# The last two passes of a graph network: selecting by products against turning rows and scanning

## The reference

```python
def _gcn_layer(x, W, b, src, dst, norm, n_nodes):
    xt = x @ W
    msg = xt[src] * norm[:, None]
    agg = jax.ops.segment_sum(msg, dst, num_segments=n_nodes)
    return jax.nn.relu(agg + b)
norm = edge_weight * jax.lax.rsqrt(deg_out[src] * deg_in[dst] + EPS)
h6 = _gcn_layer(h5_all, W6, b6, src, dst, norm, N_NODES)
h7 = _gcn_layer(h6, W7, b7, src, dst, norm, N_NODES)
out = h7 @ Wp + bp
```

## Time and profile before

| | us |
|---|---|
| median of 3 runs | 5989.73 |
| profiled execution, span from the first to the last instruction | 5993.1 |
| fifth pass, POOL's first gather to the start of the last pass | 412.1 |
| last pass, to the end | 588.7 |
| PE busy over the span | 4608.6 (77%) |
| DVE busy | 4603.5 (77%) |
| POOL busy | 3500.3 (58%) |
| ACT busy | 2965.7 (49%) |

### The profile page before, as it was taken

The page is one execution under the profiler, slowest core; times in us unless marked ns, Lnnn a source line. Parts: engine busy times, 40 slices in busy tenths (PEclk is TensorE's granted clock), DMA queues, the critical chain, the costliest instruction groups (busy, mean ns, idle before and its releaser), DMA issues. The chain is left out here.

```text
span 5993.1 us, 77451 instructions
## 1 busy us (share of the span) xinstructions
PE 4608.6 (77%) x21160; PEld 3351.9 (56%) x21160; DVE 4603.5 (77%) x13478; ACT 2965.7 (49%) x7524; POOL 3500.3 (58%) x3009
## 2 busy tenths in 40 slices
PE   3888888888884888865777778888857674887887
PEld 3666666666663666643565545555534443665555
DVE  5888888888886888847999647777768887985554
ACT  2777777777772444432444435555545552331111
POOL 3555445454524767728888278777725433546777
PEclk9999999999996999987888889999978887998998
DMA  3666666667663444425777535555536774554444
GB/s 119 239 242 247 237 243 241 244 242 244 240 236 128 125 123 129 128 71 174 256 243 250 200 110 155 147 151 155 154 103 217 249 241 151 169 159 132 140 156 130
DMA packets 651621, 1096.83 MB, mean 183 GB/s; under 512 B 88390, under 2 KB 471814, under 8 KB 651069
## 3 DMA queue, kind: packets, MB, share of 16 engines
q1 hardware_dynamic: 525754, 837.10, 41.0%
q0 software_dynamic: 125440, 254.79, 14.7%
HBM read 523.88 MB, written 575.95 MB: 184 GB/s over the span
## 5 line engine op out<-in xcount | busy, mean ns | idle before, releaser
L830 PE MATMUL mm<-w,tt 128*128 128x264 f32 x3136 | 736.9, 389 | 0.8 <-ACT tt L874 0.8
L830 PEld LDWEIGHTS mm<-w,tt 128*128 128x128 f32 x3136 | 585.5, 192 | 92.5 <-ACT tt L874 1.0
L1318 POOL DMA_INDIRECT aim<-F,index x392 | 551.7, 1407 | 119.5 <-issue 119.2
L768 POOL DMA_INDIRECT xd<-in_x_dram,index x196 | 218.4, 1114 | 676.0 <-DMA XD<-xd 645.1
L1318 POOL DMA_INDIRECT got<-F,index x392 | 491.9, 1255 | 204.7 <-issue 111.2
L1476 ACT ACTIVATE rows<-acc 128x260 f32<-128x260 f32 (+1 forms) x588 | 227.4, 387 | 623.4 <-PE acc L1467 623.4
L796 POOL DMA_INDIRECT place<-PLACE,place_ix x392 | 425.2, 1085 | 119.5 <-issue 119.5
L820 PE MATMUL tp<-ident,h 128*128 128x128 f32 x1568 | 236.8, 284 | 323.9 <-ACT h L914 162.0
L1463 PE MATMUL acc<-got,sel 128*128 128x260 f32 (+1 forms) x1176 | 425.8, 449 | 74.8 <-DVE sel L1438 68.2
L2487 DVE SCALAR_TENSOR_TENSOR agg<-mask,agg,acc 128x128 f32<-128x128 f32 x784 | 251.8, 343 | 253.5 <-PE acc L2474 144.2
L830 PE MATMUL mm<-wl,tt 128*128 128x264 f32 x1568 | 419.4, 389 | 6.0 <-ACT tt L874 5.8
(11 more groups left out here) (348 smaller groups left out, 13645.7 us busy)
## 6 DMA issues: line engine op xcount, KB each, us to landing
F<-f1o SPq DMA_DIRECT2D x97, 528.0 KB
F<-f2o SPq DMA_DIRECT2D x97, 528.0 KB, 3.4
HL<-ho SPq DMA_DIRECT2D x97, 528.0 KB, 3.7
xin<-in_x_dram SPq DMA_DIRECT2D x97, 512.0 KB
H<-h SPq DMA_DIRECT2D x97, 512.0 KB, 3.7
X<-x3o SPq DMA_DIRECT2D x97, 512.0 KB
out_dram<-oo SPq DMA_DIRECT2D x97, 512.0 KB
drow<-DSTF SPq DMA_DIRECT2D x84, 448.0 KB
```

The lines of the kernel that those rows point to most:

```text
L768: nc.gpsimd.indirect_dma_start(out=xd[:, n % 2, t, :], out_offset=None, in_=x, in_offset=bass.IndirectOffsetOnAxis(ap=index[:, tile, 1:2], ...
L830: last = nc.tensor.matmul(mm[PAIR[stage, q]][:, r, 0:F2W], lhs[:, q, 2 * r + k, :], w[:, k, :], start=(k == 0), stop=(k == KB - 1))
L1318: nc.gpsimd.indirect_dma_start(out=buf[:, n % SLOTS, t, :], out_offset=None, in_=table, in_offset=bass.IndirectOffsetOnAxis(ap=index[:, n ...
```

## The change

In both passes `sel`, `mask` and the accumulating products go. PE turns the gathered rows with its transpose into PSUM (`turned`, 128 x 512 for each half), and DVE sums along the row with one scan per half: state = same x state + turned, where `same` is 1 if the edge has the target of the edge before it, else 0. It is computed once in the set-up, kept in DRAM as SAME, and loaded in the place of `drow`. The norm is no longer in `sel`: ACT scales the rows by it, in the fifth pass after the relu, in the last right after the gather. `got` has three buffers instead of two. In the fifth pass the three Newton steps go; POOL raises the variance to the power -0.5 (L2533 of the new kernel), behind the gathers of the next group. The lags change: in the fifth pass the groups of PE are n-1 and n-3 (n-2 and n-4 before), in the last pass POOL scatters n-3 (n-4 before), and PE turns n ahead of the products of n-1 and n-2.

```diff
+def variance(nc, link, st, mean, dm, var, ready):
+
+
+    V = nc.vector
+    V.tensor_tensor(mean, st[:, :, 1], st[:, :, 4], ALU.add)
+    n = link.go(V.tensor_tensor(dm, st[:, :, 1], st[:, :, 4], ALU.subtract))
+    k = link.go(V.scalar_tensor_tensor(var, st[:, :, 2], D * 1e-5, st[:, :, 5], ALU.add, ALU.add))
+    link.need(n)
+    n = link.go(V.scalar_tensor_tensor(dm, dm, 0.25, dm, ALU.mult, ALU.mult))
+    link.need(n)
+    V.scalar_tensor_tensor(var, var, 1.0 / D, dm, ALU.mult, ALU.add).then_inc(ready, 1)
...
-                    V.memset(dst_before[:, 0:1], -1.0)
-                    V.tensor_copy(dst_before[:, 1:T], tmp[:, 0:T - 1])
...
+                    link(V.tensor_tensor(same[:, :, 1:P], rows[1][:, :, 1:P], rows[1][:, :, 0:P - 1], ALU.is_equal))
...
-                self.got = self.sb("got", [P, 2, G, D])
+                self.got = self.sb("got", [P, SLOTS, G, D])
...
+            def control(self, sp, n):
+
+                hold(sp, self.done["agg"], (n - 1) * KB, None)
+                sp.dma_start(self.same[:, n % 2, :], SAME[n * G:(n + 1) * G, :].rearrange("t p -> (t p)")
+                             .partition_broadcast(P)).then_inc(self.ctl_in[n % 2], 16)
...
-                drow = self.drow[:, sl, :].rearrange("p (t q) -> p t q", t=G)
-                for t in range(G):
-                    col = bass.ds(at.n * G + t, 1)
-                    V.tensor_scalar(self.sel[:, sl, t, :], drow[:, t, :], dst_col[:, col], norm[:, col],
-                                    ALU.is_equal, ALU.mult)
-                V.tensor_tensor(self.mask[:, sl, :, :], drow,
-                                dst_before[:, bass.ds(at.n * G, G)].unsqueeze(2).to_broadcast([P, G, P]),
-                                ALU.is_equal).then_inc(self.done["sel"], 1)
...
-                    last = nc.tensor.matmul(self.acc[sl][:, t, k, :], values[:, sl, t, k * P:(k + 1) * P],
-                                            self.sel[:, sl, t, :], start=True, stop=True)
...
+            def turn_rows(self, pe, n, values, slot):
+                hold(pe, self.done["agg"], (n - 1) * KB, None)
                 for k in range(KB):
+                    for t in range(G):
+                        last = nc.tensor.transpose(self.turned[n % 2][k][:, t * P:(t + 1) * P],
+                                                   values[:, slot, t, k * P:(k + 1) * P], ident[:, :])
+                    last.then_inc(self.done["turned"], 1)
...
-                    last = nc.vector.scalar_tensor_tensor(self.agg[:, sl, k, t * P:(t + 1) * P],
-                                                          self.mask[:, sl, t, :], before,
-                                                          self.acc[sl][:, t, k, :], ALU.mult, ALU.add)
...
+            def running_sums(self, dve, n, used, count):
+
+
+                sl = n % 2
+                hold(dve, self.ctl_in[sl], 16 * (n // 2 + 1), None)
+                hold(dve, used, count, None)
                 for k in range(KB):
+                    hold(dve, self.done["turned"], n * KB + (k + 1), None)
+                    hold(dve, self.done["agg"], (n - 1) * KB + (k + 1), None)
+                    nc.vector.tensor_tensor_scan(self.agg[:, sl, k, :], self.same[:, sl, :], self.turned[sl][k][:, :],
+                                                 self.agg[:, 1 - sl, k, G * P - 1:G * P], ALU.mult, ALU.add)\
+                        .then_inc(self.done["agg"], 1)
...
+                    def group(n):
+                        if grouped(n):
+                            ph.gather(pool, n, bound, d["relu"], n - 2)
+                        r = n - 1
+                        if grouped(r):
+                            hold(pool, d["relu"], r - 1, None)
+                            hold(pool, d["var"], r + 1, None)
+                            nc.gpsimd.tensor_tensor(rt[:, r % 2, :], var[:, r % 2, :], half[:, :], ALU.pow)\
+                                .then_inc(d["root"], 1)
+                    every_group(1, group)
...
+                        if n % 8 == 0:
+                            link.restart()
+                        b = n - 2
+                        if grouped(n):
+                            ph.gathered(dve, n)
                             for t in range(G):
+                                last = V.bn_stats(st[:, t, :], ph.got[:, n % SLOTS, t, :])
                             link(last)
+                            variance(nc, link, st, mean[:, :], dm[:, :], var[:, n % 2, :], d["var"])
+                        if grouped(b):
+                            ph.running_sums(dve, b, d["m6"], (b - 1) * 2)
+                        if grouped(n):
+                            hold(dve, d["relu"], n - 1, None)
+                            hold(dve, d["root"], n + 1, None)
+                            V.scalar_tensor_tensor(nm[:, n % 2, :], mean[:, :], -0.5, rt[:, n % 2, :],
+                                                   ALU.mult, ALU.mult).then_inc(d["stats"], 1)
+                    every_group(2, group)
...
-                        b, c = at.back(2), at.back(4)
+                        b, c = n - 1, n - 3
...
+                        c = n - 3
+                        if grouped(n):
+                            sl = n % 2
+                            hold(act, d["stats"], n + 1, None)
+                            hold(act, d["turned"], (n - 1) * KB, None)
                             for r in range(G):
+                                last = nc.scalar.activation(h[:, sl, r, :], ph.got[:, n % SLOTS, r, :], ACT.Relu,
                                                             bias=nm[:, sl, r:r + 1], scale=rt[:, sl, r:r + 1])
+                            last.then_inc(d["relu"], 1)
+                            hold(act, d["relu"], n + 1, None)
+                            for r in range(G):
+                                tile = n * G + r
+                                last = nc.scalar.activation(h[:, sl, r, :], h[:, sl, r, :], ACT.Copy,
+                                                            scale=norm[:, tile:tile + 1])
...
-            ph.step("m7", "yt", "mm", "xb")
+            ph.step("scaled", "m7", "yt", "mm", "xb")
...
-                        j = at.back(4)
-                        if at.alive(NG):
-                            ph.gather(pool, at, bound, d["acc"], at.n * G - G)
-                        if j.alive(NG):
-                            scatter_rows(j)
-                    unrolled(pool, NG, 4, group)
+                    def group(n):
+                        if grouped(n):
+                            ph.gather(pool, n, bound, d["turned"], (n - 2) * KB)
+                        if grouped(n - 3):
+                            scatter_rows(n - 3)
+                    every_group(3, group)
...
+                            ph.running_sums(dve, n, d["m7"], (n - 1) * KB)
...
-                        b, c, e = at.back(1), at.back(2), at.back(3)
+                        c, e = n - 1, n - 2
+                        if grouped(n):
+                            hold(pe, d["scaled"], n + 1, None)
+                            ph.turn_rows(pe, n, ph.got, n % SLOTS)
...
+                            ph.gathered(act, n)
+                            for t in range(G):
+                                tile = n * G + t
+                                last = nc.scalar.activation(ph.got[:, n % SLOTS, t, :], ph.got[:, n % SLOTS, t, :],
+                                                            ACT.Copy, scale=norm[:, tile:tile + 1])
+                            last.then_inc(d["scaled"], 1)
```

More of the change, by code:

```diff
@@ L267, in gnn_program @@
     PEN = dram("PEN", (EP + P,))
+    SAME = dram("SAME", (T, P))
     DEG = dram("DEG", (P * NCOL, 1))
@@ L456, in _ @@
                             .then_inc(s_dr, 16)
+                    for b in range(NB):
+                        r = min(T - b * P, P)
+                        sp.dma_start(SAME[b * P:b * P + r, :], same[0:r, b, :]).then_inc(s_dr, 16)
                     sp.dma_start(PEN[EP:EP + P].rearrange("(a n) -> a n", a=1), pen[0:1, 0, :]).then_inc(s_dr, 16)
@@ L2413, in __enter__ @@
                 Phase.__enter__(self)
[L2414 to L2416 removed]
+                self.same = self.sb("same", [P, 2, G * P])
                 self.agg = self.sb("agg", [P, 2, KB, G * P])
[L2418 removed]
+                self.got = self.sb("got", [P, SLOTS, G, D])
                 self.put = self.sb("put", [P, 2, G, D])
[L2420 removed]
+                self.turned = [[self.ps(f"turned{s}{k}", [P, G * P]) for k in range(KB)] for s in range(2)]
                 self.got_in = gathered_in[0]
@@ L2423, in __enter__ @@
                 self.ctl_in = self.slots("ctl_in", 2)
-                self.done = {k: self.sem(k) for k in ("start", "sel", "acc", "agg", "put")}
+                self.done = {k: self.sem(k) for k in ("start", "turned", "agg", "put")}
                 return self
@@ L2478, in carry_on @@
-            def carry_on(self, dve, at, t, steps=iter(()), each=0):
```

(36 more changed lines are left out.)

223 lines of the change are left out of this document (84 added, 139 removed).

## The result

| | median, us | runs |
|---|---|---|
| kernel before | 5992.9 | 5 (5988.1 to 6007.0) |
| changed kernel | 6037.5 | 5 (6018.2 to 6039.2) |

The ratio is 1.0062, 95% interval 1.0046 to 1.0078: about 37 us slower (the medians lie 45 apart), where the forecast was some 20 faster. A second measurement beside the experiments gave 1.0057 (1.0040 to 1.0074).

What follows compares the result with a forecast made beforehand. DVE was taken to bound the fifth pass and POOL the last; 5993.1 - 78 (fifth pass) + 61 (last pass) = 5976 us, so 5973 for a median, range 5912 to 6042 (the forecast's own 5945 to 6005).

Steps and rivals of the forecast that it cites:

- So POOL has 5.2 + 1.0 = 6.2 us and sets the step: Fifth pass: 4 gathers at 5.2 us plus the power at 1.0 set the group's time.
- the term of -78: Fifth pass: 73 us saved as groups go from 7.69 to 6.2 us, plus 5 us at the end.
- DVE 4.7 us a group: Fifth pass: DVE's remaining work plus two scans at 1.22 us each sums to 4.7 us, 5.3 with hand-overs.
- ACT's scaling: Fifth pass: 4 scalings by the norm take about 1.75 us a group.
- The power at 0.7: Fifth pass: POOL's power of 128x4 takes about 0.7 us, 1.0 with its gap, bounded by 0.3 and 2.3.
- signs named: What would show the forecast right or wrong, such as POOL's group at 6.2 us; wrong if fifth pass over 380 us.
- +61: Last pass: us lost because POOL's scatter waits for DVE's put, a group taking 12.85 us, 1.32 more.
- X: Last pass: time from a group's gathers being issued to DVE's put for the scatter of n-2, 14.5 us.
- R: Last pass: POOL's time for the scatter of n-3 and gathers of n+1, 11.2 us including 0.8 for xb.
- The scan as a second SBUF operand: Both passes: if a scan's start value counted, POOL blocked up to 1 us a group, +49 us each; forecast says no.
- Rival 5: Fifth pass: something shared, the DMA engines, holds a group near 7.2 us; about 6020, or 5990 if milder; chance 0.06.
- rival 2: Last pass: same scatter wait, dearer, a group 13.6 to 14.4 us; total 6008 to 6045; chance 0.20.

Runs made afterwards that it cites:

- e1: Changed kernel with SyncE storing a group's rows one group earlier (n-4, not n-5) in the fifth pass; 5978.5 us, ratio 0.9985.
- e8: Changed kernel with the store of group n-5 issued ahead of the 0/1 row's load in the fifth pass; 6029.6 us, ratio 0.9916, slower chip.
- e12: Kernel with both lags changed (store n-4, scatter n-4), with the fifth pass's power done twice in each group; 5937.2 us.
- e7: Changed kernel with ACT scaling only one of four tiles of a group in the last pass; 5987.7 us.
- e2: Changed kernel with GpSimd scattering 4 groups behind the gathers instead of 3 in the last pass; 5935.4 us, ratio 0.9901.
- e4: Kernel before with GpSimd scattering 3 groups behind the gathers instead of 4 in the last pass; 6097.0 us, ratio 1.0174.
- after: The changed kernel itself, without further edits, as profiled after the change; median 6037.5 us, ratio 1.0062 to the kernel before.
- e5: Changed kernel with the power on GpSimd done twice in each group of the fifth pass; 6063.1 us.
- e9: Kernel with both lags changed, with PE instead of DVE adding the bias in the last pass; 6009.2 us, slower chip.
- e6: Kernel with both lags changed, with the fifth pass's power done twice in each group; 6023.7 us, an earlier run than e12's.
- e3: Changed kernel with both lags changed: fifth-pass store at n-4, last-pass scatter at n-4; 5890.0 us, ratio 0.9833.

## Why the prediction was wrong

**The step that failed** is in the fifth pass: "So POOL has 5.2 + 1.0 = 6.2 us and sets the step; every other engine is below it." I added up each engine's work and never followed SyncE's queue, which has hardly any work and still holds the step. There the store of n-5 stands behind a load that waits for the scans of n-2. In the changed kernel both lie on one loop (load, store, put, products, turn, scan, load). With the fall of PE's clock that it brings, it makes the group 7.6 us on average, and the term of -78 came out at -16 and -32. e1 and e8, which put the store ahead of that load and change nothing else, give 338 and 345 us; the term had said 336.

**Step by step:**
- DVE 4.7 us a group, ACT's scaling, PE's turns: right (scan 1.27, four scalings 1.7, 8 turns 1.0).
- The power at 0.7: too low, 1.04 with a gap of 0.2, so 1.24 where 1.0 was counted with the gap. The bound of 0.3 to 2.3 held it. e12 shows that it counts once the store is in time.
- Of the signs named, POOL's group of 6.2 us showed only with the store in time (e1), and ACT's waits for nm were up to 2.5 us even there, not under 1. The pass stayed over 380 us, which the prediction had named as wrong.
- The last pass: mechanism right, the term a little large: +61 against +51 and +57. X was 14.5 against 14.2 and R 11.2 against 10.7. e7 confirms that half of a change in X shows, e2 that POOL takes over where X is covered. PE's clock fell from 0.91 to 0.88, as named, and over the whole pass the scatters waited 102.5 us for put, within the 60 to 150.
- The same sum doesn't fit the old order: it gives X as 11.7 us there, and e4 was expected 20 us slower. e4's group of 13.6 us would ask for an X near 15.7 (2 x 13.6 - 11.5, an estimate). Where those 4 us lie stays open.
- The scan as a second SBUF operand: the row's answer stands. In after, gathers begun inside scans of the fifth pass take 1.00 us (5193.49, 5194.79).
- Rival 5 had the right place and size (a group near 7.2, about 6020) but the wrong cause: it named the DMA engines, whose share is 0.53 in after and 0.61 in e1, where the pass is 60 us shorter. Its 0.06 was far too little.
- The range, 5912 to 6042, held the time, but by luck: it reached so far up for rival 2, a last pass at +95 or more, and that did not come. The miss of 46 to 62 us lies in the fifth pass.

## What to carry to other kernels

When the work of the bounding engine is taken away, write down every queue that issues in order, the idle DMA queue above all, and ask of each wait in it what stands behind. Here a store whose data was ready stood behind a load, and a buffer of two slots did the rest; moving it cost nothing and gave 43 and 57 us, each on one chip. A lag between issue and consumption is cover: here each us on the path cost about half a us a group (e7), and in the old order one group of lag cost five times what the sum said (e4). So recompute it whenever a step (here the scaling and the turn) goes in front of it.

## What the runs showed of the hardware

- After 3.55 us of idle time PE's granted clock was 0.50 (5201.5 to 5207.3) and pairs of products took 1.06 us, not 0.59. After 4.86 us 8 turns took 1.78, after 2.38 us 1.09 (5682.44).
- A power of 128x4 on GpSimd takes 1.04 us, about as much as an indirect DMA's issue, though four values per partition are next to nothing.
- One store in the same place of the queue made PE wait up to 3.7 us and fall to the lower clock where POOL needs 6.3 us a group (after), and cost nothing where POOL needs 7.3 (e5).
- With DVE's sum of two SBUF operands gone, POOL's gathers and scatters took 1.01 and 1.00 us on average (e9); with it 1.04 and 1.10 (e6, same chip).
- Two chips ran the kernel before 80 us apart (5995 and 6075). Of kernels with the same last pass, e8's took 645.3 us on the slow one and e1's 644.2 on the other, while the faster last pass of e6 and e3 took 605.9 and 556.0.
